# One graph layer, one core: the skip projection joined to the node projection and stored in a sums table; two sums tables in place of four

## What is computed

```python
h = jnp.maximum(_layernorm(x, axis=-1), 0.0)
s, v = h[:, :64], h[:, 64:].reshape(N, 32, 3)
skip_s, skip_v = s @ W_skip0, jnp.einsum('nmi,mk->nki', v, W_skip1)   # 96 + 96 columns
s, v = s @ W_nl0, jnp.einsum('nmi,mk->nki', v, W_nl1)                 # 64 + 96 columns
w = jax.nn.relu(edge_feature @ W_fc1) @ W_fc2                         # 224 per edge
xs, xv = s[dst], v[dst]
# tp: products of w, xs, xv and the edge's unit vector (dot and cross products)
agg = jax.ops.segment_sum(tp, src, num_segments=N) / 32
out_s = agg[:, :96] @ W_out_s + skip_s
out_v = jnp.einsum('nmi,mk->nki', agg_v, W_out_v) + skip_v
x = x + concat(silu(out_s[:, :64]), sigmoid(out_s[:, 64:96]) * out_v)
```

## Time and profile before

| | us |
|---|---|
| three runs | 1494.34, 1494.89, 1687.11 |
| their median | 1494.89 |
| profiled execution, first to last instruction (span) | 1490.1 |
| median less span | 4.8 |
| busy: POOL / PE / DVE / ACT | 1134.9 / 1184.7 / 891.4 / 451.2 |

### The profile page before, as it was taken

One profiled execution on the slowest core, in us unless ns is written; L12 is line 12 of the kernel. 1 busy time (PEld: TensorE's weight loads), 2 busy tenths in 40 slices (PEclk: granted clock), 3 DMA queues, 4 the chain that ended last, 5 costly groups with the idle time before them and its releaser, 6 DMA issues.

```text
span 1490.1 us, 23307 instructions
## 1 busy us (share of the span) xinstructions
PE 1184.7 (80%) x5766; PEld 975.6 (65%) x5766; DVE 891.4 (60%) x3688; ACT 451.2 (30%) x868; POOL 1134.9 (76%) x853
## 2 busy tenths in 40 slices
PE   8889788787887879788787878889787887878800
PEld 5668667676766667677676767767676776767700
DVE  6429556665656666555566656556665656666519
ACT  4234323233332323323232332323232232332300
POOL 1417888888888888888888888888888888888864
PEclk7559967778777877868777786877787687786855
DMA  5444545545454544545445454544545454554574
GB/s 225 153 154 95 96 79 91 84 77 98 75 93 83 89 86 77 98 75 93 82 87 88 75 100 75 92 83 86 90 76 99 75 91 84 84 90 69 68 195 158
DMA packets 118198, 144.09 MB, mean 97 GB/s; under 512 B 30880, under 2 KB 91552, under 8 KB 118176
## 3 DMA queue, kind: packets, MB, share of 16 engines
q0 software_dynamic: 79872, 75.03, 36.0%
q1 hardware_dynamic: 36576, 61.34, 13.1%
q10 hardware_dynamic: 1728, 7.47, 1.2%
HBM read 88.56 MB, written 55.21 MB: 96 GB/s over the span
## 4 chain that ended last, share of the span: by engine, by line
issue 29%; POOL 27%; DMA 24%; PE 11%; DVE 7%; POOLq 1%; DVEq 1%; ACT 0%; ACTq 0%
DMA sums<-to_add,add_idx 19%; POOL rows L302 16%; POOL sums L320 11%; DMA rows<-node_table,to_idx 4%; PE o_ps L460 2%; PE w_ps L427 2%; DVE products_space L757 1%; DVE products_space L728 1%; PE t_ps L442 1%; PE d_ps L475 1%; PE d_ps L398 1%; DVE products_space L755 1%; PE d_ps L396 1%; PE o_ps L396 1%; PE o_ps L398 1%
## 5 line engine op out<-in xcount | busy, mean ns | idle before, releaser
L320 POOL DMA_INDIRECT sums<-to_add,add_idx x416 | 678.1, 1630 | 126.7 <-issue 118.8
L302 POOL DMA_INDIRECT rows<-node_table,to_idx x416 | 424.6, 1021 | 193.9 <-issue 119.3
L728 DVE TENSOR_TENSOR products_space<-rows,rhat 128x256 f32<-128x256 f32 (+2 forms) x520 | 170.3, 394 | 506.2 <-DMA rows<-node_table,to_idx 506.2
L460 PEld LDWEIGHTS o_ps<-w,pT 128*128 128x128 f32 (+1 forms) x2496 | 414.2, 252 | 40.1 <-issue 32.8
L460 PE MATMUL o_ps<-w,pT 128*128 128x96 f32 (+1 forms) x2496 | 431.3, 340 | 0.0
L442 PE MATMUL t_ps<-w,products_space 128*128 128x128 f32 (+1 forms) x1248 | 237.7, 324 | 213.6 <-DVE products_space L757 208.0
L442 PEld LDWEIGHTS t_ps<-w,products_space 128*128 128x128 f32 (+1 forms) x1248 | 182.2, 171 | 233.4 <-issue 221.9
L427 PE MATMUL w_ps<-w,hid 64*128 64x224 f32 x832 | 283.6, 475 | 0.8 <-ACT hid L568 0.7
L576 ACT ACTIVATE pT<-t_ps 128x512 f32<-128x512 f32 (+1 forms) x312 | 185.2, 594 | 262.0 <-PE t_ps L442 239.0
L585 ACT ACTIVATE msg<-o_ps 128x448 f32<-128x448 f32 x208 | 113.0, 543 | 409.9 <-PE o_ps L460 364.4
L427 PEld LDWEIGHTS w_ps<-w,hid 64*128 64x128 f32 x832 | 180.7, 240 | 59.3 <-issue 49.2
(11 more groups left out here) (115 smaller groups left out, 557.7 us busy)
## 6 DMA issues: line engine op xcount, KB each, us to landing
from_row<-nodes_row SPq DMA_DIRECT2D x52, 512.0 KB
ef<-edge_t SPq DMA_DIRECT2D x52, 256.0 KB
rows<-node_table,to_idx POOLq DMA_INDIRECT x416
sums<-to_add,add_idx POOLq DMA_INDIRECT x416
sums<-zeros ACTq DMA_DIRECT2D x8, 672.0 KB
sums<-zeros SPq DMA_DIRECT2D x4, 672.0 KB
x_sb<-x SPq DMA_DIRECT2D x5, 400.0 KB, 6.6
node_table<-node_rows SPq DMA_DIRECT2D x5, 400.0 KB, 2.4
```

Of the source, the lines that this page charges most:

```text
L302: pool.indirect_dma_start(rows[:, u, j, SC:CR], None, table, bass.IndirectOffsetOnAxis(ap=to_idx[:, par, h * J + j:h * J + j + 1], axis=0) ...
L320: pool.indirect_dma_start(sums[j], bass.IndirectOffsetOnAxis(ap=add_idx[:, u, j:j + 1], axis=0), to_add[:, u, j, :], None, compute_op=ALU.add,
L460: ins = nc.tensor.matmul(o_ps[m][:, base + oc:base + oc + n], pT[c][u % 2][:, cols], w[0:ROWS[c], wc:wc + n], start=(q == 0 and c == 0), s ...
L728: ins = nc.vector.tensor_tensor(vecs(crs[:, dst, :, i0 * V:(i0 + n) * V], n), vecs(rows[:, u, :, VE + v0 * V:VE + (v0 + n) * V], n), unit( ...
```

## The change

- `project_node` now makes all 352 columns of a tile at once: the scalar product is 160 columns wide (96 skip, 64 node), the vector product 192 (96 node, 96 skip). ACT copies 352 columns a tile to `node_out`, scaled as before. `skip_products`, `copy_skip` and the waits for them are gone.
- After every 5 tiles SP writes the middle 160 columns to `node_table` as before, and then with two more DMAs the outer 96 + 96 to `sums_0`. So table 0 begins with the skip and not with zeros. Zeros go to table 1 (4 DMAs) and to the 128 spare rows of table 0 (1 DMA), all on SP's queue.
- There are two tables. Scatters 0 and 2 of a group go to table 0, scatters 1 and 3 to table 1, and each waits for the landing of the scatter two before it in the order.
- The last stage loads two tables (12 DMAs in place of 24), each only after both of its last scatters have landed. DVE does one addition a piece; POOL does nothing there.

```diff
@@ -64,11 +64,9 @@
 LAST = [slice(a, min(a + n, NT)) for a, n in ((0, 5), (5, 5), (10, 5), (15, 5), (20, 3), (23, 2))]
-SKIP_PAIRS = -(-NT // 2)
+TABLES = 2
 ZR = 7
 ZERO_RUNS = [(a, min(a + ZR, TABLE_ROWS // P)) for a in range(0, TABLE_ROWS // P, ZR)]
@@ -83,7 +81,7 @@
-    sums = [nc.dram_tensor(f"sums_{j}", [TABLE_ROWS, M], F32, kind="Internal").ap() for j in range(J)]
+    sums = [nc.dram_tensor(f"sums_{j}", [TABLE_ROWS, M], F32, kind="Internal").ap() for j in range(TABLES)]
@@ -100,8 +98,7 @@
-        node_rows = sb("node_rows", [P, NT, F])
-        skip = sb("skip", [P, NT, M])
+        node_out = sb("node_out", [P, NT, S + M + 3 * V])
@@ -161,33 +158,24 @@
-        part = [flat[:, 0:J * CH * M].rearrange("p (j t m) -> p j t m", j=J, t=CH)
-                for flat in (h_sb[:, :, :].rearrange("p a b -> p (a b)"),
-                             rows[:, :, :, :].rearrange("p u j f -> p (u j f)"),
-                             node_rows[:, :, :].rearrange("p t f -> p (t f)"),
-                             hT[:, :, :, :].rearrange("p t a b -> p (t a b)"),
-                             products_space[:, :])]
-        part.append(part[0])
+        spent = node_out[:, :, :].rearrange("p t f -> p (t f)")
+        spent_h = h_sb[:, :, :].rearrange("p t f -> p (t f)")
+        size = TABLES * CH * M
+        part = [flat[:, k * size:(k + 1) * size].rearrange("p (j t m) -> p j t m", j=TABLES, t=CH)
+                for flat, k in ((spent, 0), (spent, 1), (spent, 2), (spent, 3), (spent_h, 0), (spent_h, 1))]
-        def set_zero(engine, j, a, e):
-            engine.dma_start(sums[j].rearrange("(p t) m -> p t m", p=P)[:, a:e, :],
-                             zeros[:, 0:e - a, :]).then_inc(zeroed, 16)
@@ -227,13 +215,17 @@
             sp.wait_ge(zero_set, 1)
-            for part_of_sums in ZERO_PARTS[:EARLY_ZEROS]:
-                set_zero(sp, *part_of_sums)
+            for a, e in ZERO_RUNS:
+                sp.dma_start(sums[1].rearrange("(p t) m -> p t m", p=P)[:, a:e, :],
+                             zeros[:, 0:e - a, :]).then_inc(zeroed, 16)
+            sp.dma_start(sums[0][NPAD:TABLE_ROWS, :], zeros[:, 0, :]).then_inc(zeroed, 16)
                 sp.wait_ge(rows_ready, (c + 1) * CH)
-                sp.dma_start(table_d[:, step_of(c), :], node_rows[:, step_of(c), :]).then_inc(table_out, 16)
+                sp.dma_start(table_d[:, step_of(c), :], node_out[:, step_of(c), SO:SO + F]).then_inc(table_out, 16)
+                sp.dma_start(sums_d[0][:, step_of(c), 0:SO], node_out[:, step_of(c), 0:SO]).then_inc(skip_out, 16)
+                sp.dma_start(sums_d[0][:, step_of(c), SO:M], node_out[:, step_of(c), SO + F:]).then_inc(skip_out, 16)
             load_to(2, 0, 1)
@@ -248,22 +240,17 @@
-            def load_sums(c, tables):
-                if c == 3:
-                    sp.wait_ge(skip_ready, SKIP_PAIRS)
-                if c == 5:
-                    sp.wait_ge(out_ready, 1)
-                for j in tables:
-                    if c == 0:
-                        sp.wait_ge(added[j], 16 * GROUPS)
-                    n = LAST[c].stop - LAST[c].start
-                    sp.dma_start(part[c][:, j, 0:n], sums_d[j][:, LAST[c], :]
-                                 ).then_inc(fourth_in[c] if j == J - 1 else three_in[c], 16)
-            for c, tables in ((0, [0]), (1, [0]), (0, [1]), (0, [2]), (1, [1, 2]), (0, [3]), (1, [3])):
-                load_sums(c, tables)
-            for c in range(2, len(LAST)):
-                load_sums(c, range(J))
+            def load_sums(c, j):
+                n = LAST[c].stop - LAST[c].start
+                sp.dma_start(part[c][:, j, 0:n], sums_d[j][:, LAST[c], :]).then_inc(tables_in[c], 16)
+            for j in range(TABLES):
+                sp.wait_ge(added[j], 16 * GROUPS)
+                sp.wait_ge(added[j + 2], 16 * GROUPS)
+                load_sums(0, j)
+            for c in range(1, len(LAST)):
+                for j in range(TABLES):
+                    load_sums(c, j)
             for c, tt in enumerate(LAST):
@@ -312,13 +299,17 @@
                     pool.wait_ge(sums_ready, 2 * g + 1 + j // 2)
-                if valid(g - 1, GROUPS):
-                    pool.wait_ge(added[j], 16 * g)
+                if j >= TABLES:
+                    pool.wait_ge(added[j - TABLES], 16 * (g + 1))
+                    tick()
+                elif valid(g - 1, GROUPS):
+                    pool.wait_ge(added[j + TABLES], 16 * g)
                     tick()
                 else:
-                    pool.wait_ge(zeroed, 16 * len(ZERO_PARTS))
+                    pool.wait_ge(zeroed, 16 * (len(ZERO_RUNS) + 1))
+                    pool.wait_ge(skip_out, 16 * 2 * STEPS)
                 pool.indirect_dma_start(
-                    sums[j], bass.IndirectOffsetOnAxis(ap=add_idx[:, u, j:j + 1], axis=0),
+                    sums[j % TABLES], bass.IndirectOffsetOnAxis(ap=add_idx[:, u, j:j + 1], axis=0),
@@ -341,17 +332,6 @@
-            pool.wait_ge(skip_ready, SKIP_PAIRS)
-            for c, tt in enumerate(LAST):
-                pc = part[c][:, :, 0:tt.stop - tt.start]
-                pool.wait_ge(three_in[c], 16 * 3)
-                nc.gpsimd.tensor_tensor(pc[:, 2], pc[:, 2], skip[:, tt, :], ALU.add).then_inc(with_skip, 1)
-                if c < len(LAST) - 1:
-                    pool.wait_ge(with_skip, c + 1)
-                    pool.wait_ge(fourth_in[c], 16)
-                    nc.gpsimd.tensor_tensor(pc[:, 2], pc[:, 2], pc[:, 3], ALU.add).then_inc(half_sum, 1)
@@ -374,9 +354,9 @@
                     pe.wait_ge(rows_ready, t - 3)
-                nc.tensor.matmul(op[:, 0:S], hT[0:S, t, 0, :], w[0:S, W_NS + SO:W_NS + SO + S],
+                nc.tensor.matmul(op[:, 0:SO + S], hT[0:S, t, 0, :], w[0:S, W_NS:W_NS + SO + S],
                                  start=True, stop=False, skip_group_check=True)
-                nc.tensor.matmul(op[:, S:F], hT[0:3 * V, t, 1, :], w[0:3 * V, W_NV:W_NV + 3 * V],
+                nc.tensor.matmul(op[:, SO + S:SO + S + 6 * V], hT[0:3 * V, t, 1, :], w[0:3 * V, W_NV:W_NV + 6 * V],
                                  start=False, stop=True, skip_group_check=True).then_inc(projected, 1)
@@ -384,21 +364,6 @@
...
-            def skip_products(n):
...
-                for q, t in enumerate(tiles):
-                    nc.tensor.matmul(bank[:, q * M:q * M + SO], hT[0:S, t, 0, :], w[0:S, W_NS:W_NS + SO],
-                                     start=(q == 0), stop=False, skip_group_check=True)
-                    ins = nc.tensor.matmul(bank[:, q * M + SO:(q + 1) * M], hT[0:3 * V, t, 1, :],
-                                           w[0:3 * V, W_NV + 3 * V:W_NV + 6 * V], start=False,
-                                           stop=(t == tiles[-1]), skip_group_check=True)
-                ins.then_inc(skip_done, 1)
@@ -449,8 +414,6 @@
                     pe.wait_ge(pT_ready, 3 * g + 3)
-                if isinstance(g, int) and g == 0:
-                    pe.wait_ge(skip_ready, SKIP_PAIRS)
                 if valid(g - 1, GROUPS):
@@ -491,9 +454,6 @@
                 merge(g - 3, u3, 1)
-                if isinstance(g, int) and g == 0:
-                    for n in range(SKIP_PAIRS):
-                        skip_products(n)
@@ -526,7 +486,7 @@
                 act.wait_ge(projected, t + 1)
-                nc.scalar.activation(node_rows[:, t, :], (o_ps + w_ps)[t % 4][:, 0:F], ACT.Copy,
+                nc.scalar.activation(node_out[:, t, :], (o_ps + w_ps)[t % 4][:, 0:SO + S + 6 * V], ACT.Copy,
                                      scale=node_std[:, 1, t:t + 1]).then_inc(rows_ready, 1)
@@ -544,21 +504,6 @@
-            def copy_skip(n):
-                for q, t in enumerate(range(2 * n, min(2 * n + 2, NT))):
-                    ins = nc.scalar.activation(skip[:, t, :], (d_ps, o_ps[0])[n % 2][:, q * M:(q + 1) * M], ACT.Copy,
...
-                ins.then_inc(skip_ready, 1)
-            later_zeros = ZERO_PARTS[EARLY_ZEROS:]
...
-            def next_zeros(i):
-                if isinstance(i, int) and later_zeros:
-                    set_zero(act, *later_zeros.pop(0))
@@ -601,22 +546,14 @@
                 copy_turned(g - 1, u1, 0)
-                next_zeros(i)
                 copy_outputs(g - 2, u2, 0)
                 copy_turned(g - 1, u1, 1)
-                next_zeros(i)
                 collect(g - 3, u3, 0)
...
                 copy_turned(g - 1, u1, 2)
-                next_zeros(i)
                 if u % 2 == 1:
                 collect(g - 3, u3, 1)
-                if isinstance(g, int) and g == 0:
-                    for n in range(SKIP_PAIRS):
-                        copy_skip(n)
-                        if n % 4 == 0:
-                            next_zeros(1)
@@ -856,18 +793,8 @@
                 pc = part[c][:, :, 0:tt.stop - tt.start]
-                dve.wait_ge(three_in[c], 16 * 3)
-                nc.vector.tensor_tensor(pc[:, 0], pc[:, 0], pc[:, 1], ALU.add).then_inc(pair_sum, 1)
...
```

(17 more changed lines are left out.)

18 lines of the change are left out of this document (removed).

## The result

The changed kernel took 1452.77 us (median of its four runs: 1448.57, 1450.38, 1455.16, 1474.01), the kernel before 1494.62 us beside it: ratio 0.9722, 95% interval 0.9687 to 0.9758. The time lies in the predicted range, 9 us above the forecast of 1444 and just outside the forecast's own range of 1436 to 1452. The profiled execution took 1455.16 us with a span of 1453.4, so 36.7 us of span went where 51 were forecast: by the span the forecast of 1439 was 14 us too low.

A forecast was written before the change was run, and what follows sets the result against it. POOL issuing gathers and scatters was taken as the bound, 1353 of the 1490.1 us span. Terms -26.9 - 11 + 1 + 3 + 0 + 9 - 26 = -51 made span 1439, with 4.8 around it 1444 us; range 1433 to 1470.

The forecast's parts named there:

- The hole: Start: with the skip products removed, the 26.9 us DVE waited for group 1's `fc2` go: -26.9 us.
- the fill: Start: PE idles for the first gathers, so the first groups' work may begin at half clock: +3 us, bounds 0 and +12.
- The node stage: Start: wider products bring most of the stage to the upper clock level, about 19 tiles from 1.7 to 1.05 us: -11 us.
- stores: Start: skip writes and 640-byte table pieces on SP beside the first gathers: +1 us, bounds -2 and +4.
- stays at half: Rival, start: the node stage stays at the 1.2 GHz level, 1459 us; chance 0.22.
- The extra 3 us: Start: if skip pieces of 384 B took double time, some 3 us more before the first gather, 1447 us.
- The loop: Loop: waiting for the scatter two before costs nothing, 4.3 us needed against 6.38: 0 us, bounds 0 and +10.
- the slower rival: Rival, loop: scatter landings of 6.52 us become the limit over 208 pairs, +193 us, 1637 us; chance 0.08.
- The last 28 scatters: End: scatters without gathers wait for the one two before, 0.64 us more for each of 14 pairs: +9 us.
- The last stage: After the last scatter: two tables loaded, one DVE addition a piece, 26.5 us in place of 52.6: -26 us.
- The 4.8 us around the span: Whole execution: time outside the profiled span, 4.8 us, added to the forecast span of 1439 us.
- The start isn't handed on: Rival, start: POOL waits for the first groups' chain, so half of the 26.9 us stays, 1457 us; chance 0.10.

The follow-up runs named there:

- e12: The changed kernel unedited, run a third time, on the third chip: 1438.87 and 1439.06 us in the two executions compared.
- e4: The changed kernel with three POOL memsets (about 11 us) ahead of the first gathers: 1458.43 us.
- e2: The changed kernel with four sums tables again, each scatter waiting for the one four back, three additions a piece on DVE: 1450.15 us, ratio 0.9815 to the kernel before.
- e1: The kernel before with node-stage products made 160 and 192 wide, skip stage left in: 1475.4 us, ratio 0.9959 to the kernel before.
- e7: The changed kernel with every scatter into table 0, each waiting for the one just before it: 2054.14 us, ratio 1.387.
- e8: The changed kernel with a POOL memset of 1.22 us ahead of each of the first 28 gathers: 1469.75 us.
- e5: The changed kernel unedited, run again on the second chip: 1450.22 us, ratio 0.9787 to the kernel before there.
- e6: The kernel before, skip stage kept, with two tables and the last stage's additions on DVE alone: 1480.31 us, ratio 0.9978 to the kernel before.
- e3: The changed kernel with 18 matmuls of 512 columns, results unused, after group 0's `fc2`: 1453.22 us.
- the light pace: The changed kernel with POOL memsets of 576 elements a partition ahead of the 16 gathers of groups 3 to 6: 1447.61 us, ratio 0.9859.

## Why the prediction was right, and where it was off

**The hole (-26.9) and the fill (+3).** This is the step that missed: together -24 forecast, -10.7 measured. "Group 1's `fc2` then comes when its inputs are there" was right as a mechanism (no skip row, POOL's hole of 25.74 gone, and e12 has the fill in 39.8 us, 27.0 less than before). The size was off in the execution profiled, for two things. The idle time of 26.94 us was taken whole as the skip's, though PE itself was idle in 5.2 us of it; and the fill at half level lasted until 104, in the outer part of my 0 to +12. The two holes of POOL, 11.83 and 7.03 us less the usual 0.30 each, are 18.3 us of the fill's 56.1.

**What the stall is stays open.** It isn't a fixed moment (e4), nor the clock's level (e2, e12), and it isn't tied to the skip work, since it is in both kernels. It stood in the profiled executions of both kernels and of e1 to e7, and in none of e8 to e12, the last four on one chip. It was seen while gathers were issued back to back. Whether the pace in e8 removed it or chance did, one run can't tell, and e12 shows that an unpaced execution can be without it. I don't know which resource holds PE's result back.

**The node stage (-11, stores +1).** Right in kind: 0.95 in place of 0.50, and e1 shows the joined products as its cause. -7.1 for -10, since a tile took 1.21 us and not 1.05: some 19 x 0.16 = 3 us, which is the difference. The rival "stays at half" is out. The stores: the table of the changed kernel came 0.8 us after that of e1 (first gather 44.75 and 43.95), which writes no skip rows; I had taken 1. With 44.49 in e5 and 44.13 in e12 it is 0.2 to 0.8, on three chips. The extra 3 us that I worked out by the Trainium skill, DMA: Bandwidth & Descriptors, section "Specifications", for pieces under 512 B did not appear. The pieces may be slower all the same: in the changed kernel's trace a skip write of 240 KB landed 3.7 us after its issue (median), a table write of 400 KB after 2.8. The last skip writes are issued behind the last table write, so the first gather doesn't wait for them.

**The loop (0).** Right: -2.1 in this trace, and 1263.3 with four tables in e2, so the slower rival is out. e7 confirms landing plus restart at 4.4 us for a scatter by itself, against 6.38 available.

**The last 28 scatters (+9).** Right: +9.7, and +9.1 in e6, -9.7 when undone in e2.

**The last stage (-26).** Right, and by its terms: the second load was in 7.5 us after the last scatter, where I had 8.5, and DVE took 18.6 us, where I had 18. Together 26.1 us in place of 52.6. e6, the same stage with the skip tile added, also has DVE's first addition 7.5 us after the last scatter.

**The 4.8 us around the span.** This term was mis-sized. In every execution recorded with its span the time is 1.8 us above it (1455.16 and 1453.4 in the profiled one); the 4.8 was the difference of a median and the span of another execution. By 1.8 the sum would have given 1441. So the 9 us between forecast and time are smaller than the 14 on the span for reasons that the prediction can't claim: 3 us from this term, and some from the profiled execution being the slowest of the three compared.

**How large the gain is.** 42 us is the largest of three chips: some 32 on e5's and 29 on e12's. The forecast of 51 is too high on each. On those two chips the kernel before is itself faster (1483 and 1468 us in the mean, 1494 on the first), so their times can't be held against 1444, only their gains.

**"The start isn't handed on"** (1457) described the time better than its mechanism: POOL's and DVE's hole was one, as I argued, and it went; what it was replaced by is the stall and the slow level, not the chain of the first groups. In e12, without the stall, the fill took 39.8 us; its time of 1439 can't be held against the forecast of 1444, since the kernel before was 26 us faster there too.

## What to carry to other kernels

Before a hole is booked as the gain of removing the work in it, see whether every engine in it is really working: here PE stood idle for 7 us in the work that was to go, 5 of them in the hole, and a stall of that length was in the changed kernel's trace too. Cut the span at a few instructions of the limiting engine and account between them; changes of opposite sign (+10 and -26 at the end) show there and cancel in the total. And profile the unchanged kernel beside every variant on the same chip: the light pace looked like a cure until the unpaced kernel ran next to it and was 8 us faster. Read a clock level in the stretch where the event lies: a mean over 13 or 26 us hid that e3's stall began at half.

## What was unexpected of the hardware

A result of PE reached ACT some 7 us late (end of the product by its record 68.07, start of the copy 75.17, releaser "remote") with no work on any engine to explain it, once in the fill; nine of fourteen profiled executions have such a stall, and the same program ran without it on another chip. Between those two traces of the changed kernel lie 16 us of span, all of it in the fill; how much of that is the stall and how much the low clock behind it no run separates. The stage of 64- and 96-column products stayed at the 1.2 GHz level for 32 us with PE busy throughout (two traces of two), and the same stage with 160 and 192 columns was at 0.94 to 1.00 (twelve of twelve). The same addition of 128 x 960 on DVE took 3.14 us beside POOL's additions and 1.16 us without them. A chain of dependent accumulating scatters of 128 rows of 768 B runs at one per 4.4 us, of which 3.5 are landing and 0.8 to 0.9 restart; independent ones follow at 1.86 us.
